# VectorE forms the gate product ahead of the low halves in the expert stage of a decoder layer

## The reference, cut to what matters

```
h1 = einsum('btd,edc->btec', x, w1_routed)       # 256 -> 176
h2 = einsum('btd,edc->btec', x, w3_routed)       # 256 -> 176
h3 = silu(h1 * h2)                               # the gate product h1*h2, then silu
experts_out = einsum('btec,ecd->bted', h3, w2_routed)     # 176 -> 256
routed_out  = einsum('bted,bte->btd', experts_out, router_probs)
```

## Time and profile before

| | |
|---|---|
| time of the profiled execution | 816.65 us |
| its span, first to last instruction | 814.9 us |
| median of the three runs | 812.66 us (808.79 to 813.05) |
| first, last gate product | 486.72 us, 800.72 us from the span's start |
| granted clock of TensorE, 488 to 799 us | 1.00 |
| matmul, VectorE, ScalarE busy, 541 to 799 us | 257.91, 197.82, 151.59 of 258.00 us |

### The profile page before, as it was taken

How to read it: one execution, slowest core, us unless ns; L and a number is a source line. 1 busy time by engine, 2 the same in 40 slices (tenths; PEclk the granted TensorE clock), 3 DMA queues, 4 the chain that set the end, 5 groups by cost and what they waited for, 6 DMA issues and landing times. The chain is left out here.

```text
span 814.9 us, 15783 instructions
## 1 busy us (share of the span) xinstructions
PE 656.4 (81%) x4034; PEld 550.8 (68%) x4034; DVE 568.8 (70%) x1747; ACT 402.9 (49%) x1136; POOL 461.1 (57%) x363
## 2 busy tenths in 40 slices
PE   0887689886358789798756627899999999999994
PEld 0776578665345556665544326799999999999993
DVE  5899967961667566666464757777777777777773
ACT  3977356311336435453323326556565656555552
POOL 3555765462002644546556624677777776877775
PEclk9999989999579989899988659999999999999997
DMA  9910100031234366453324643577878776877874
GB/s 289 294 38 26 40 14 27 27 116 39 98 123 145 129 213 220 161 193 122 113 88 155 204 131 72 105 132 132 131 130 132 133 131 113 145 131 131 133 113 57
DMA packets 77094, 100.38 MB, mean 123 GB/s; under 512 B 9744, under 2 KB 70304, under 8 KB 76448
## 3 DMA queue, kind: packets, MB, share of 16 engines
q0 software_dynamic: 26736, 37.64, 26.2%
q1 hardware_dynamic: 48096, 59.64, 23.9%
q10 hardware_dynamic: 2176, 2.10, 0.9%
HBM read 50.97 MB, written 52.95 MB: 128 GB/s over the span
## 5 line engine op out<-in xcount | busy, mean ns | idle before, releaser
L1562 POOL DMA_INDIRECT out_dram<-yw,xg x143 | 225.2, 1574 | 109.4 <-issue 54.0
L1184 POOL DMA_INDIRECT xs_scratch<-rows,slot x128 | 125.9, 984 | 146.6 <-issue 72.7
L1445 PE MATMUL cbank<-w_hi,xtc_hi 128*128 x286 | 107.5, 376 | 7.6 <-DVE xtc_lo L1457 7.5
L1445 PE MATMUL cbank<-w,stc_hi 112*128 (+1 forms) x572 | 112.3, 289 | 1.0 <-DVE stc_hi L1527 0.8
L1505 ACT ACTIVATE sgc<-hh 128x128 f32<-128x128 f32 x143 | 44.4, 311 | 129.7 <-DVE hh L1499 91.5
L1457 DVE TENSOR_TENSOR xtc_lo<-cbank,xtc_hi 128x256 fp32r<-128x256 f32 x143 | 60.6, 424 | 60.7 <-ACT xtc_hi L1452 50.2
L355 POOL TENSOR_TENSOR pv<-v_sb,pr 128x256 f32<-128x256 f32 (+7 forms) x32 | 68.5, 2155 | 57.4 <-DVE pr L344 40.9
L1445 PEld LDWEIGHTS cbank<-w,stc_hi 112*128 112x128 f32 (+1 forms) x572 | 92.1, 189 | 6.3 <-issue 3.3
L1445 PE MATMUL cbank<-w,xtc_hi 128*128 x286 | 93.3, 326 | 0.0
L1445 PE MATMUL cbank<-w_hi,xtc_lo 128*128 x286 | 92.6, 324 | 0.0
L1445 PEld LDWEIGHTS cbank<-w_hi,xtc_hi 128*128 128x128 f32 x286 | 54.1, 189 | 22.9 <-issue 10.7
(11 more groups left out here) (223 smaller groups left out, 1562.9 us busy)
## 6 DMA issues: line engine op xcount, KB each, us to landing
xg<-xs_scratch SPq DMA_DIRECT2D x143, 144.0 KB
w<-w13r_dram SPq DMA_DIRECT2D x8, 704.0 KB
w_hi<-ctx_t_dram SPq DMA_DIRECT2D x8, 512.0 KB
x_scratch<-x_all SPq DMA_DIRECT2D x16, 256.0 KB, 2.1
w_hi<-x_scratch SPq DMA_DIRECT2D x8, 512.0 KB, 4.1
out_dram<-w SPq DMA_DIRECT2D x16, 256.0 KB
w<-w2r_dram SPq DMA_DIRECT2D x4, 1024.0 KB
x_all<-x_dram SPq DMA_DIRECT2D x12, 256.0 KB
```

Of the source, the lines that this page charges most:

```text
L1184: nc.gpsimd.indirect_dma_start(t["xs"], bass.IndirectOffsetOnAxis(ap=slot[:, n % 2, k:k + 1].bitcast(U32), axis=0), rows[:, n % NROW, k // ...
L1445: last = nc.tensor.matmul(out, stationary, moving, start=j == 0, stop=j == len(pairs) - 1)
L1562: nc.gpsimd.indirect_dma_start(t["out"], bass.IndirectOffsetOnAxis(ap=xg[:, p, ID:ID + 1].bitcast(U32), axis=0), yw[:, p % YB, :], None, c ...
```

## The change

In `plan` the key of `s_lo_` on VectorE goes from 0.7 to 1.3. It stood between `t_lo` (0.2) and `hh_` (1.2); it now stands between `hh_` and `y_ev` (4.1). Nothing else is changed: the same instructions, the same tiles, the same waits and buffers. "Two steps older" is the tile whose low halves are made: the gate product is that of tile i-4, the low halves those of tile i-6. The order on TensorE, ScalarE, GpSimd and SyncE is what it was.

```
-                (0.5, "t", 6, s_t), (0.6, "s", 6, s_hi_), (0.7, "v", 6, s_lo_),
+                (0.5, "t", 6, s_t), (0.6, "s", 6, s_hi_), (1.3, "v", 6, s_lo_),
                 (1, "t", 4, h_mm), (1.1, "s", 4, h2_), (1.2, "v", 4, hh_), (1.3, "s", 4, sg_),
                 (4, "t", 7, y_mm), (4.1, "v", 7, y_ev)]
```

## The result

The changed kernel takes 784.77 us (median of 783.57, 785.45, 788.03 and 784.08), the kernel before 812.31 us on the same footing (four runs, 808.79 to 813.05). The ratio is 0.968, with a 95% interval of 0.965 to 0.971: 25.8 us less, give or take 2.2 (the two medians alone differ by 27.5). The profiled execution of the changed kernel took 783.57 us, its span is 781.8 us.

What follows compares the result with a forecast made beforehand. The prediction took a closed 2.15 us loop of VectorE and ScalarE waits, not TensorE, to bound the kernel. Gains of 15.1 + 6.2 - 1.0 = 20.3 us from a median of 812.66 gave 792.5 us, range 785 to 804.

Steps and rivals of the forecast that it cites:

- The ring: VectorE and ScalarE wait for each other from `t_lo` to the next `t_lo`; 2.15 us falls to 1.53.
- Rivals A: TensorE is as full as its busy time says, the 0.14 us no wait; 806.5 us, chance 0.07.
- D: Rival: ScalarE's silu waits for something else, such as copy `h2_`, so nothing changes; 812 us, chance 0.03.
- Two of the signs given: Profile after: gate product 0.34 us behind `t_lo`; ScalarE's idle time moved from in front of silu to in front of `h2_`.
- TensorE as next bound: Long part, from tile 12 on: TensorE sets 2.035 us a tile instead of 2.152, gaining 15.1 us.
- the slow steps: TensorE rounds now and then 0.12 us slower, estimated one tile in eight; 0.015 us a tile charged.
- The other chains fit: Copy, gate product and low halves take 1.25 of 1.84 us before `y_mm`, leaving 0.6 us to spare.
- rival C: Low halves come late for `y_mm`, so TensorE stands there in every tile; slower, 832.5 us, chance 0.04.
- The early part: Tiles 1 to 11: pace falls from 3.004 to 2.38 us a tile, gaining 6.2 us.
- The scatters: GpSimd's scatters at 1.94 us a tile fit under 2.035 but leave a small debt at the end: -1.0 us.
- rival B: The scatters set the pace and VectorE waits for buffers, costing up to 8 us; 800 us, chance 0.06.
- The debt: Scatters' lag of some 3 us after tile 83's wait; clears in 15 tiles before the change, 30 to 40 after.

Runs made afterwards that it cites:

- e3: Kernel before with two of the five `y_mm` matmuls left out; ratio 0.999 to the kernel before.
- e5: Changed kernel, but only the second low half goes behind the gate product, the first staying ahead of it; 787.57 us, ratio 0.971 to the kernel before.
- e6: Kernel before with the first low half computed twice on VectorE; 836.7 us, ratio 1.032 to the kernel before.
- e10: Changed kernel with the split of the second weights moved behind the copy on ScalarE and behind the low halves on VectorE; ratio 0.968 to the kernel before.
- e4: Changed kernel with two of the five `y_mm` matmuls left out; ratio 0.951 to the kernel before.
- e7: Changed kernel with the low halves also moved behind `y_ev` (key 4.2 in place of 1.3); ratio 1.007 to the kernel before.
- e8: Kernel before with the gate product moved ahead of `t_lo` (key 1.2 to 0.15); ratio 1.040 to the kernel before.
- e9: Changed kernel run once more unaltered, beside two variants on one chip; ratio 0.969 to the kernel before.

## Why the prediction was right, point by point

1. *The ring* held. It was read as 2.15, became short, and e3 (no matmul matters), e5 (one moved low half suffices in the long part) and e6 (an added term lengthens it) have the marks of a ring of two engines without TensorE; its length after the change, 1.53 us, is seen in e10's first step. Rivals A (e3) and D are out with it. Two of the signs given did not come in the long part: the gate product is 0.73 behind `t_lo`, not 0.34 (that is so only in the early part, 504.32 to 504.65), and ScalarE's idle time moved only in part, 0.41 of 0.89 us staying in front of silu and 0.23 standing in front of the copy. Both follow from TensorE setting the pace: the gate product waits for a copy that waits for `h_mm`. The 0.34 is a distance of the ring, and in the long part the ring no longer decides.
2. *TensorE as next bound* was right as a mechanism (e4) and undersized as a term. Forecast were 2.035 us a tile and 15.1 us; measured 2.005 and 0.147 x 129 = 18.9 us, over the 18.3 given as bound. The difference is made of these: the hand-over is 0.27, not the middle of 0.27 and 0.30 (0.01), and the trace of before already has 0.27 in some rounds; the rest of TensorE's round is 1.73 in place of 1.74 (0.01); and the slow steps, for which 0.015 was charged, are gone. From second `h_mm` matmul to the next last transpose, 21 of 124 rounds before took over 1.80 us; none of 120 after takes over 1.75. They were taken for TensorE's own cost, which the wait absorbed. The traces show that they came with the wait: behind each `h_mm` TensorE's queue reads the number of the next expert from the table (L1463), 0.30 us in the median, at times up to 0.7. Before, that load starts 0.02 to 0.25 us behind the start of the second matmul; all 21 slow rounds have a load of 0.41 us or more, and none of the rounds under 1.75 has one over 0.45. After, it starts 0.3 to 0.45 us ahead of the second matmul, 26 loads take 0.46 to 0.71 us, and no round is longer for it. No run took the load away.
3. *The other chains fit*, and rival C didn't come. The forecast counted 0.6 us of room to the first matmul of `y_mm`, and 0.62 is measured there; counted to its weight load, which is what waits in e7, it is 0.46, so the sum was right and its end was put 0.16 us too late. The hand-over from gate product to low half, which no row of before had, is 0.26. The argument was thinner than it looked, though: e7 shows that one place further down, behind `y_ev`, the same instructions close another ring.
4. *The early part* gave 10 x 0.62 = 6.2 us, exactly the term. That is not luck: the pace was read off the one step of before in which no low half existed yet.
5. *The scatters* lost 0.6 us behind the stage, against 1.0 forecast, and rival B didn't come: from 515 to 765 us VectorE waits for the copy alone. The wait at tile 83 came again, 3.11 us, and at tile 104 a second one, 2.18 us, that the kernel before doesn't have:

```profile
655.42 1.55 POOL L1562 DMA_INDIRECT out_dram<-yw,xg  x1 [0.30 <-issue]
660.09 1.55 POOL L1562 DMA_INDIRECT out_dram<-yw,xg  x1 [3.11 <-SPq L1421]
...
701.87 1.55 POOL L1562 DMA_INDIRECT out_dram<-yw,xg  x1 [2.18 <-SPq L1421]
```

The debt lasted longer than the 30 to 40 tiles forecast, for another reason than the small slack: scatters start 4.41 us behind the end of `y_ev` at tile 85 and 2.35 at 99, 0.15 less with each tile (2.005 - 1.86). Forecast was 0.10, because every eighth step was to cost more, which it doesn't while they are late. Then the wait at 104 and another behind it bring it back to 4.36 at 105, and it is at the usual 0.83 only at tile 132. Why an earlier scatter lands too late for tile 104 is open. The 0.6 us isn't this debt, which is paid back by then. In both kernels a wait stands ahead of the scatter of tile 136, and from there to the last one the scatters take 11.14 us, at their shortest step, however fast the tiles come. That the term came out near its forecast is luck in part.

The sum with the measured terms is 18.9 + 6.2 - 0.6 = 24.5 us; the gap between tiles 11 and 12 and the last steps add the 0.3 that bring it to the stage's 24.8. The measured ratio gives 25.8, and 1 us of that is within its interval. The forecast's own upper bounds, 18.3 + 7, make 25.3, so the stage's gain lies within them; the best value was low because the term of the long part was undersized by 3.8 us. That the median of the runs fell 2.7 us more than the stage did, and so just under the range, no run explains; in the profiled executions the stages ahead differ by up to 17 us.

## What to carry to other kernels

In a pipeline of engines that each work in a fixed order, look for rings: follow one instruction back through releasers and queue neighbours until it comes round, and add start-to-start times. If the sum is the pace, no other engine bounds the kernel, however busy it looks; shorten the ring to just under the next bound and stop, for another place in the order (e7, e8) can build a ring through that next engine. Count the room of a moved instruction to the weight load that needs it, not to the matmul. To test whether an engine is the bound, take some of its work away and see if the pace moves.

## What the runs showed of the hardware

A wait of 0.14 us a tile left no idle time on TensorE's row: the matmul that waited showed 0.42 us against 0.32, and its predecessor's drain covered the rest. A matmul that turns from transposes to weights shows 0.41 even without a wait, so the start of the second matmul is the one to read. A load of one number from the table into TensorE's queue, of 0.41 us or more in place of 0.30, lengthened TensorE's round while it stood behind the matmuls, and not once the queue ran ahead of them. Executions reached the same point, the first gate product, at 478 to 496 us (the changed kernel at 478.41 and, in e9, at 488.83), while the stage behind it repeated to 0.1 us (288.6 twice): comparing inside a stage told 2 us apart where whole times could not. And of VectorE's instructions that start at one partition the next starts 0.08 us before the last one ends, but one that reads and writes from partition 64 gives up that overlap on both its sides: it starts 0.01 us behind the end of the one ahead, and the next one 0.04 behind its own, which costs 0.09 and 0.12 us. With its own 0.21 that is 0.42, the 3.004 - 2.581 by which e5, which moves that instruction alone, shortens the early ring.
